# A feed-forward bias moved from TensorE to GpSimd in an attention and feed-forward kernel

## The reference

```python
def _L0_ffn_ref(x, weight, bias):
    w_scale = jnp.mean(jnp.abs(weight))
    q_weight = jnp.sign(weight) * (jnp.abs(weight) > 0.5 * w_scale).astype(weight.dtype)
    i_scale = jnp.max(jnp.abs(x)) / 127.0
    q_input = jnp.clip(jnp.round(x / i_scale), -128.0, 127.0)
    out = jnp.einsum('bsk,ok->bso', q_input, q_weight) * w_scale * i_scale
    out = out + bias
    return out

x = x + _L0_xattn_ref(_layernorm(x, axis=-1), ctx_1024, L0_xattn_Wq, L0_xattn_Wk, L0_xattn_Wv, L0_xattn_Wo)
x = x + _L0_ffn_ref(_layernorm(x, axis=-1), L0_ffn_weight, L0_ffn_bias)
```

## Time and profile before

| | |
|---|---|
| median of 3 runs | 1374.23 us (1371.97 to 1374.83) |
| span of the profiled execution (first to last instruction) | 1373.2 us |
| mean granted clock of TensorE | 0.989 |
| VectorE, ScalarE, GpSimd busy | 86%, 75%, 58% of the span |

### The profile page before, as it was taken

The page is one execution under the profiler, slowest core; times in us unless marked ns, Lnnn a source line. Parts: engine busy times, 40 slices in busy tenths (PEclk is TensorE's granted clock), DMA queues, the critical chain, the costliest instruction groups (busy, mean ns, idle before and its releaser), DMA issues.

```text
span 1373.2 us, 36872 instructions
## 1 busy us (share of the span) xinstructions
PE 1326.4 (97%) x9911; PEld 1075.1 (78%) x9911; DVE 1185.1 (86%) x2772; ACT 1028.5 (75%) x2338; POOL 793.1 (58%) x1534
## 2 busy tenths in 40 slices
PE   5898999999999999999999999999699999999998
PEld 5787999999999999999999999998344444444443
DVE  4876999999999999999999999999677777777776
ACT  3454788888888888888888888888567767766765
POOL 3564888888888888888888888888100000000000
PEclk9999999999999999999999999999799999999999
DMA  8674355465564555645555523321089999999744
GB/s 260 177 214 130 84 182 168 157 193 153 171 187 143 186 165 159 192 150 174 177 151 189 163 72 99 100 71 35 31 302 347 344 349 348 347 345 350 292 183 184
DMA packets 100815, 265.18 MB, mean 193 GB/s; under 512 B 49705, under 2 KB 65769, under 8 KB 72114
## 3 DMA queue, kind: packets, MB, share of 16 engines
q1 hardware_dynamic: 100786, 264.86, 58.5%
HBM read 139.64 MB, written 125.17 MB: 193 GB/s over the span
## 4 chain that ended last, share of the span: by engine, by line
DVE 46%; PE 33%; issue 14%; DMA 3%; DVEq 2%; SPq 1%; ACT 1%; POOL 1%; POOLq 0%; ACTq 0%
PE bank L1245 18%; DVE amax L895 9%; DVE x_sb L927 7%; PE bank L1243 6%; DVE e_sb L941 6%; DVE mx_sb L937 5%; DVE bn_sb L886 5%; PE bank L1236 4%; DVE qT_sb L909 2%; DVE rinv_sb L883 2%; DVE ve_sb L915 2%; DVE bn_sb L878 1%; DVE mv_sb L901 1%; DMA x_sb<-in_ctx 1%; PE bank L1062 1%
## 5 line engine op out<-in xcount | busy, mean ns | idle before, releaser
L716 ACT ACTIVATE x_sb<-bank,mean,cols 128x512 f32<-128x512 f32 x256 | 198.2, 774 | 120.0 <-DVE x_sb L1002 77.8
L1245 PE MATMUL bank<-wT,x_sb 128*128 128x512 f16 x1024 | 267.4, 384 | 0.0
L1165 PE MATMUL bank<-wqs,xT_sb 128*128 128x128 f32 x2048 | 260.3, 280 | 0.6 <-ACT xT_sb L638 0.5
L1165 PEld LDWEIGHTS bank<-wqs,xT_sb 128*128 128x128 f32 x2048 | 238.7, 192 | 7.4 <-ACT xT_sb L638 1.2
L1213 PE MATMUL bank<-v_blk,pT_sb 103*128 103x136 f32 x1536 | 199.0, 279 | 0.3 <-ACT pT_sb L680 0.3
L1213 PEld LDWEIGHTS bank<-v_blk,pT_sb 103*128 103x128 f32 x1536 | 190.6, 189 | 0.5 <-ACT pT_sb L680 0.5
L927 DVE SCALAR_TENSOR_TENSOR x_sb<-x_sb,negm,bank 128x512 f32 (+1 forms) x256 | 179.6, 743 | 6.3 <-PE bank L1176 2.7
L895 DVE TENSOR_REDUCE amax<-x_sb (+1 forms) x128 | 156.0, 1219 | 23.2 <-DVE bn_sb L886 8.0
L689 ACT ACTIVATE sq_sb<-x_sb 128x512 bf16 (+1 forms) x256 | 161.4, 631 | 18.7 <-DVE x_sb L927 1.4
L1245 PEld LDWEIGHTS bank<-wT,x_sb 128*128 128x128 f16 x1024 | 79.5, 98 | 120.0 <-issue 60.0
L994 DVE TENSOR_SCALAR x_sb<-bank 128x1024 f16<-128x1024 f16 x128 | 88.5, 692 | 97.0 <-PE bank L1236 97.0
(11 more groups left out here) (124 smaller groups left out, 2612.2 us busy)
## 6 DMA issues: line engine op xcount, KB each, us to landing
out_y<-x_sb SPq DMA_DIRECT2D x112, 1024.0 KB, 4.8
x_sb<-in_x SPq DMA_DIRECT2D x64, 1024.0 KB, 6.4
x_sb<-out_y SPq DMA_DIRECT2D x48, 1024.0 KB, 6.7
x_sb<-in_ctx SPq DMA_DIRECT2D x38, 256.0 KB, 2.9
k_blk<-k_scr SPq DMA_DIRECT2D x256, 19.2 KB, 5.5
k_scr<-x_sb SPq DMA_DIRECT2D x38, 128.0 KB, 2.3
v_scr<-x_sb SPq DMA_DIRECT2D x38, 68.0 KB, 2.4
v_blk<-v_scr SPq DMA_DIRECT2D x128, 10.2 KB
```

The source lines that it names most:

```text
L716: act.activation(u_sb[:, t, :], bank[4 + t][:, :], ACT.Identity, bias=stat_of(mean1, j, t, back), scale=cols[:, 6:7]).then_inc(scaled_t, 1)
L1165: last = pe.matmul(bank[2][:, t * HD:(t + 1) * HD], xT_sb[:, t, c, :], wqs[:, c, :], start=c == 0, stop=c == EC - 1)
L1245: last = pe.matmul(bank[4 + t][:, :], q16T_sb[:, t, c, :], wT[:, c, :], start=False, stop=c == EC - 1)
```

## The change

The bias matmul and all that prepares it are taken out. The bias is loaded once, repeated over 128 partitions, into the space of `xT_sb` when the last projection is done. In the last stage GpSimd adds it in place to the rows of a batch in `x1_sb`, two tiles in an instruction (128x1024), as soon as both of these tiles have been quantised. VectorE's `add` waits for that (`biased`) as well as for `scale_out`.

```diff
-        bones = sb("bones", [BR, P], BF16)
-        brow = sb("brow", [BR, E], BF16)
+        bias_sb = xT_sb[:, 0, :, :].rearrange("p c r -> p (c r)")
...
@@ SP
-                    sp.dma_start(fbias, fb.unsqueeze(0).broadcast_to([BR, E])).then_inc(fb_in, 16)
...
                 kv_step(b, b % XS)
 
+            sp.wait_ge(q_done, NP_)
+            sp.dma_start(bias_sb, fb.unsqueeze(0).broadcast_to([P, E])).then_inc(fb_in, 16)
+
             def result_out(g, k, b):
...
@@ GpSimd
             steps(pool, step)
+
+            pool.wait_ge(fb_in, 16)
+
+            def add_bias(g, k):
+
+                j = g * XS + k
+                for m, read in enumerate((quant_01, quant_23)):
+                    pool.wait_ge(read, 2 * j + 2)
+                    half = x1_sb[:, bass.ds(x1_turn(g, k) + 2 * m * E, 2 * E)].rearrange("p (t e) -> p t e", t=2)
+                    pool.tensor_tensor(half, half, bias_sb.unsqueeze(1).broadcast_to([P, 2, E]),
+                                       ALU.add).then_inc(biased, 1)
+
+            for k in range(XS):
+                add_bias(0, k)
+            with pool.Fori(1, B // XS) as g:
+                for k in range(XS):
+                    add_bias(g, k)
...
@@ VectorE, context stage, steps 9 to 12
-                elif j == 9:
-                    then(dve.tensor_reduce(rcol[:, 0:3], ident[0:BR, 0:BR].rearrange("p (a b) -> p a b", a=3),
-                                           AX.X, ALU.add))
...
@@ VectorE, between the stages
-            a, a1, a2, part, row = (cols[0:BR, 3:4], rcol[:, 6:7], rcol[:, 7:8], a16[:, :], rcol[:, 3:4])
-            mids(dve.reciprocal(a, cols[0:BR, 6:7]))
...
-            dve.tensor_scalar(bones[:, :], ones_sb[0:BR, :], row, None, ALU.mult).then_inc(bias_ready, 1)
-
+            dve.wait_ge(scale_ready, 1)
...
@@ VectorE, last stage
             def add(g, k, t):
 
-                dve.wait_ge(scaled_t, (g * XS + k) * TPB + t + 1)
+                j = g * XS + k
+                dve.wait_ge(biased, 2 * j + t // 2 + 1)
+                dve.wait_ge(scaled_t, j * TPB + t + 1)
...
@@ TensorE
-                pe.matmul(bank[4 + t][:, :], bones[:, :], brow[:, :], start=True, stop=False)
                 for c in range(EC):
-                    last = pe.matmul(bank[4 + t][:, :], q16T_sb[:, t, c, :], wT[:, c, :], start=False,
+                    last = pe.matmul(bank[4 + t][:, :], q16T_sb[:, t, c, :], wT[:, c, :], start=c == 0,
                                      stop=c == EC - 1)
...
             q_T(0, 1)
-            pe.wait_ge(bias_ready, 1)
```

More of the change, by code:

```diff
@@ L64 @@
 ZEROED = 5
-BR = 9
 CHEAD = 16
@@ L166, in build @@
         wT = sb("wT", [P, EC, E], F16)
-        bones = sb("bones", [BR, P], BF16)
-        brow = sb("brow", [BR, E], BF16)
-        rcol = sb("rcol", [BR, 8])
-        a16 = sb("a16", [BR, 1], BF16)
         at = [PARTS]
@@ L201, in build @@
         wo_t = early(D)
-        fbias = early(E)[0:BR, :]
-        bpart16 = early(E // 2).bitcast(BF16)[0:BR, :]
         fw_sb = early(EC, E)
@@ L257, in build @@
         bn_step, mv_ready, mean_ready = sem("bn_step"), sem("mv_ready"), sem("mean_ready")
-        mid, var_ready, rs2_ready, scale_T, scale_row, scale_B, scale_ready, bias_ready = (
+        mid, var_ready, rs2_ready, scale_T, scale_row, scale_B, scale_ready = (
             sem(n) for n in ("mid", "var_ready", "rs2_ready", "scale_T", "scale_row", "scale_B",
-                             "scale_ready", "bias_ready"))
-        quant_01, quant_23, qT2_done, qT2_copied, ffn_done_t, scaled_t, sum_done_t = (
-            sem(n) for n in ("quant_01", "quant_23", "qT2_done", "qT2_copied", "ffn_done_t", "scaled_t", "sum_done_t"))
+                             "scale_ready"))
+        quant_01, quant_23, qT2_done, qT2_copied, ffn_done_t, scaled_t, sum_done_t, biased = (
+            sem(n) for n in ("quant_01", "quant_23", "qT2_done", "qT2_copied", "ffn_done_t", "scaled_t", "sum_done_t",
+                             "biased"))
         def at_least(eng, s, n):
```

## The result

The changed kernel takes 1532.1 us (median of 4 runs, 1530.3 to 1535.1) where the kernel before takes 1374.0: a ratio of 1.115, 95% interval 1.114 to 1.117. The profiled execution spans 1531.1 us. It lies in the predicted range; the predicted time was 1497.

The account below looks back on a forecast made before the run. TensorE was taken to bound the last stage at 6.04 us a turn. 62 x (8.08 - 6.04) = 126.5 us, less 3.3 and 0.2, gives 123 on the median of 1374.2: 1497 us, range 1400 to 1545.

Parts of the forecast that it names:

- The exclusion: Last stage: GpSimd's adds and VectorE's four two-SBUF-tensor adds and two quantisations a turn wait for each other: 7.47 to 8.69 us.
- GpSimd's add: Last stage: two added 128x1024 adds a turn, taken at 2.35 us each, with 1.87 kept for the range.
- dear rows: Trace rows of GpSimd instructions at 2.1 ns an element, extended to 2.35 us for the last stage's 128x1024 add.
- cheap rows: Trace rows of GpSimd instructions at 1.64 ns an element, extended to 1.87 us for the last stage's 128x1024 add.
- The sum for a turn: Last stage, one batch: GpSimd 4.40, VectorE's adds 2.28, quantisations 0.79; 7.47 to 8.69 us, taken as 8.08.
- the two holds: Last stage: GpSimd's two adds a turn, 2.20 us each behind VectorE, with the VectorE operations that they block.
- The covering of `unoffset`: Last stage: whether VectorE's two PSUM-reading `unoffset`, 0.61 us each, run under GpSimd's adds; one taken as covered.
- the middle: Last stage: 8.08 us a turn, between 7.47 with both `unoffset` under GpSimd and 8.69 with neither.
- The gains outside the last stage: Context stage without the split of the bias into three bf16 rows: 3.3 us; chain for `bones` between the stages: 0.2 us.
- The load of the bias: 256 KB queued on SP behind the attention stage's loads, landing in 2.9 us, covered; uncovered about 3 us once.
- The fast rival: Last stage: port shared without loss, TensorE's turn 4.76 us, DMA next at 348 GB/s; about 1327 us, chance 0.08.
- Half clock on top: Last stage: waiting TensorE granted 1.2 GHz, needing 8.65 us a turn; bounds 1535 and about 1610 us, chance 0.07.

Follow-up runs that it names:

- the spare memory: Changed kernel with GpSimd's two adds a turn on spare memory, VectorE not waiting for them, bias left out of the output: 1502.5 us.

## Why the prediction was right, and by what it was off

- **What bounded the kernel before**: TensorE, right. Without the bias matmul and without GpSimd's adds the time falls by 84 us.
- **The exclusion**: right in kind and size. It holds with VectorE's wait gone, stays with TensorE's work put back, follows the length of GpSimd's add, vanishes for adds that read PSUM, and all of it vanishes when no VectorE operation of the two kinds is left.
- **How long one blocks the other**: the rule of the Trainium skill, page "SBUF — State Buffer", section "Who interferes with whom", agrees with the runs. VectorE's adds of two SBUF tensors stood for up to 2835 ns beside GpSimd's adds of 2.3 to 2.8 us, whole holds and not pieces; adds with one operand in PSUM kept 679 ns, as the same section has it for instructions with at most one SBUF input.
- **GpSimd's add**: 2.35 us predicted from the dear rows, 2.343 measured at the least. The cheap rows' 1.87 was not approached, not even on the spare memory (2.116). The estimate from the Trainium skill, page "GPSIMD Engine Reference", section 3.1, was 2.25 us, between the two measurements. By it the sum comes out 2 x 0.10 x 62 = 12 us lower, not the 11 stated.
- **The sum for a turn**: the two holds, grouped as the rows show them, were right one by one: 2.20 + 0.79 = 2.99 and 2.20 + 0.54 + 0.60 = 3.34 us were predicted, 2.89 and 3.35 were measured, though GpSimd's first add stands between the quantisations and not ahead of two adds. The covering of `unoffset` is the mis-sized term. I took the middle, with one `unoffset` covered, 8.08 us; neither is covered, and the prediction's own end for that was 8.69, against 8.64 measured. The reason is the hand-over: a waiting GpSimd add gets in behind one VectorE operation, here between the two quantisations and between the last two adds, and the operation that then stands in front of VectorE's queue is one that must wait. 62 x (8.64 - 8.08) = 35 us, all of the difference between 1497 and 1532. The middle was a choice without a row behind it, so the 35 us were open from the start.
- **The gains outside the last stage**: 3.5 us predicted. In the context stage the four steps that had held the split gained the predicted 3.3. What is left of it at the start of the last stage isn't shown: 2.5 us between the two traces, but two traces with the split differ by 2.4 there.
- **The load of the bias**: right. It landed 3.1 us after its issue at 945.9, and GpSimd's first add starts at 973.9.
- **TensorE and DMA fall behind**: right (DMA share 0.66 where I had some 0.72).
- **The fast rival** was mis-sized in its own terms: I had taken 348 GB/s as what DMA can give, since the engines were busy 0.97 of the time. That was the traffic which TensorE's pace asked for. DMA moves 424 GB/s when asked for it, and the rival's time would have been nearer to 1289 us, that of the run without GpSimd's adds, than to 1327. Two unhindered GpSimd adds need 2 x 2.35 = 4.7 us where that run's turn is 4.6, so by estimate it is some us more.
- **The clock**: I had said I would be wrong if it fell below 1.00 in the last stage. It did, to 0.90, with TensorE busy 63% of the time, so the argument from the earlier trace rows against *Half clock on top* failed. What kept it harmless is TensorE's room in a turn. In the changed kernel eight matmuls at 1200.19 take 1.90 us and eight of the next turn, at 1208.83, take 2.99 us, part of them at the 1.2 GHz level. The windows of the two turns, columns as in the earlier trace rows (the granted clock is 1.00 in the first and 0.80 in the second, and 0.50 from 1209.60 to 1211.20, within the second):

```profile
1199.98:1208.62 8.64, 4.69 (x32) 2.38 (x32) 8.64 (x9) 4.20 (x7) 5.26 (x2) 1.00 0.66 243
1208.62:1217.26 8.64, 6.19 (x32) 3.19 (x32) 8.64 (x9) 4.33 (x7) 5.20 (x2) 0.80 0.68 243
```

```profile
1199.98 1.28 DVE L988 TENSOR_TENSOR x_sb<-x_sb 128x512 f32 x2
...
1200.19 1.90 PE L1230 MATMUL bank<-wT,x_sb 128*128 128x512 f16 x8 [2.46 <-DVE x_sb L978]
...
1208.62 1.27 DVE L988 TENSOR_TENSOR x_sb<-x_sb 128x512 f32 x2
...
1208.83 2.99 PE L1230 MATMUL bank<-wT,x_sb 128*128 128x512 f16 x8 [3.40 <-DVE x_sb L978]
...
1217.26 1.28 DVE L988 TENSOR_TENSOR x_sb<-x_sb 128x512 f32 x2
```

Both turns, from one pair of adds to the next (1199.98, 1208.62, 1217.26), take 8.64 us, at 1.00 and at 0.80 alike.

## What to carry to other kernels

Before work is moved to GpSimd because it is idle, look at what VectorE does in that stretch: each add of two SBUF tensors and each scalar operation from SBUF (both fp32 here) takes turns with GpSimd's adds, so the two engines' times add up as if they were one engine. The remedy that the runs showed is to give VectorE operations with one operand in PSUM, and to leave the SBUF-to-SBUF work to ScalarE; then GpSimd's adds cost VectorE nothing. A DMA share near 1 isn't a proof that DMA is full; look whether transfers land later and whether anyone waits for them.

## What the runs showed of the hardware that I had not expected

- DMA at a share of 0.97 moved 348 GB/s before; with the engines faster it moved 424 at 1.01. What changed with it is the time to landing: a load of 1 MB took 6.7 us at the median on the page before, and 12.3 us in the run without GpSimd's adds.
- GpSimd's add of 128x1024 takes 2343 ns in place on the rows and 2116 ns on the spare memory. Why the place matters was not tried.
- A waiting GpSimd add is served behind one VectorE operation, also when VectorE's next one already stands in the queue: between the two quantisations at 1210.42 and the two adds at 1213.31.
